# A two-layer transformer step on one core: when three side stages of a software-pipelined kernel are issued

## The chip, the cores and the metric

The kernel runs on 1 core of one Trainium2 chip. The metric is the device time of one execution in microseconds. Five engines run their own instruction streams and meet at semaphores: PE (TensorE, matmuls; PEld is its weight load), DVE (VectorE), ACT (ScalarE), POOL (GpSimd) and SP (SyncE, which only issues DMAs).

## What is computed

Sixteen sequences of 256 tokens with 128 features pass through two layers. The reference, cut to what matters:

```python
# layer 0
xn = _layernorm(x)
s = attention(xn, Wq, Wk, Wv, Wo) + bo            # 16 heads of 64, causal softmax
idx = top_k(xn @ router, 1)                        # one of 8 experts for each token
routed = (silu(g*xn @ w1[e]) * (g*xn @ w3[e])) @ w2[e]
shared = (silu(xn @ ws1) * (xn @ ws3)) @ ws2
x = x + s * silu(shared + routed)
# layer 1
xn = _layernorm(x)
s = linear_attention(xn, ...)                      # 16 heads of 8, running sums over tokens
f = xn
for l in range(2):                                 # 8 heads of 64, window 64, rotary
    f = f + local_attention(shift(f) @ wqkv[l]) @ wo[l]
    f = f + glu(layernorm(shift(f)) @ w1[l]) @ w2[l]
x = x + s * silu(f)
```

Everything is float32.

## The kernel before

The tokens form 8 blocks `b` of 512 tokens (4 tiles of 128). The work of all blocks is laid out by `Plan.lay_out` on a common list of 322 *ticks*. A tick holds at most one attention *step* (a pair of heads for one of the two sequences of a block: kind 0 is layer 0's causal attention, kind 1 the local attention of layer 1) and a list of *side stages*. Each engine's program walks the same ticks. The order inside a tick is fixed for each engine:

- PE: `produce` (queries and keys of coming pairs: L554 for kind 0, L564 transposes for kind 1), `logits` of the tick (L574 to L587), `transposes` of the probabilities of the tick before (L595), the side stages, `values` of the tick two before (L615 for kind 1, L629/L632 for kind 0), and for every second step `merge` (L639).
- ACT: evacuation of `produce` (q, k at L849), its half of the transposed probabilities (L886), the side stages, `exps` of the tick (L871, L872), evacuation of `merge` (rT at L849).
- DVE: `masked` of the tick (L1041, reads the logits from PSUM), its half of the transposed probabilities (L1052), reciprocal (L1058), `scaled` (L1063), the side stages.
- POOL: `expand` (L1341) and then the side stages; SP: side stages that are plain DMAs.

An engine issues in order, so where a side stage stands in the list decides what waits behind it. PSUM banks are handed out in rings of two (`mm`, `s`, `pt`, `o`), in the order in which the stages stand in the plan.

The side stages that the change touches:

- `("v", b, half, t)`: the value projection of layer 0 for tile `t` and one half of the heads. PE: one 128x512 matmul (L545; the profile counts two records for each). ACT: one evacuation into `v0` (L849). For each block there are 4 tiles of half 0 and 4 of half 1. They need `xnT` of the block and must be there before the first `values` of that half.
- `("r", b)`: POOL issues four indirect DMAs (L1377) that gather the routed experts' results of the block's tokens from DRAM into `r`, which is the same buffer as `xn0`. Only `down0` reads it.
- `("down0", b)`: the down projection of the shared expert. PE: 12 matmuls (L672, 24 records); DVE adds `r` and evacuates the bank (L1094).
- `("comb", b)`: ACT takes a tanh of that sum (L915, waits for L1094); DVE forms `x + s * silu(...)` in three operations one after the other (L1100, L1102, L1104), which wait for the tanh.

`f0` and `f1` are the first ticks of the block's attention for half 0 and half 1, `c` is the tick of `down0`, `late` is 4 for blocks 3 to 6 and 0 for the others, `XRING` is 3. Blocks come 36 ticks apart from block 3 on: `f0` is 81, 117, 153, 189, 225 for blocks 3 to 7, `f1` is 97, 133, 169, 205, 241, and `c` is 116, 152, 188, 224 for blocks 3 to 6. Around them stand the side stages of layer 1 of the block ahead: `lin`, `qkv` with `mix`, `rot` and `rr` (DVE: L1227, L1231, L1236, then a chain of small operations; POOL: L1395 to L1402, L1456, L1457), `kn` (L1327), `kv` (POOL L1441, L1445), `ln2`, `ln2n` (DVE, ends with L315 on `h`), `yT` (PE L540, waits for that) and `glu` (L774, L776).

## Time and profile before

| | |
|---|---|
| median of 3 runs | 2084.16 us (2081.3 to 2085.23) |
| profiled execution | 2096.84 us, span 2095.0 us |
| mean granted TensorE clock | 0.918 |
| PE busy | 1780.8 us, 85% of the span |
| DVE busy | 1283.2 us, 61% |
| ACT busy | 1186.3 us, 57% |
| POOL busy | 868.5 us, 41% |
| PE's share of the chain that ended last | 48% |
| DVE's share of it | 20% |

Busy time is summed over one profiled execution. The chain is followed back from the last instruction to whatever released each step. Positions in the trace are microseconds from the start of the span. Tick 116 is at about 810, tick 117 at 820, tick 124 at 854 and tick 134 at 914 us; the same places of the next blocks lie some 232 us further on each.

### The profile page before, as it was taken

The numbers are of one execution on the slowest core, as the hardware profiler recorded it, in microseconds if no ns is written. First come the engines' busy times: TensorE is split into PE (matmuls) and PEld (weight loads), VectorE is DVE, ScalarE is ACT, GpSimd is POOL, SyncE is SP. The second block draws the span as 40 slices with busy tenths as digits, with TensorE's granted clock in tenths as the row PEclk, the third lists the DMA queues.
The fourth block names the chain that finished last, engine by engine and source line by source line (L and its number), as shares of the span: only waits on it lengthen the run. The fifth ranks groups of instructions, "written<-read, shape, count | busy, mean of one in ns | idle before, by whom it ended". The sixth has DMA issues, their size and how long they took to land.

```text
span 2095.0 us, 38065 instructions
## 1 busy us (share of the span) xinstructions
PE 1780.8 (85%) x12532; PEld 1150.7 (55%) x12532; DVE 1283.2 (61%) x4211; ACT 1186.3 (57%) x3527; POOL 868.5 (41%) x993
## 2 busy tenths in 40 slices
PE   6679988998989888998889988988889897785876
PEld 4358754654566455664565456554556455463554
DVE  4434446556675567566756566656756656868663
ACT  2444547565756575657656675657556565553643
POOL 2633215533535334432544344533553345646410
PEclk9889999999999999999999999999999998898978
DMA  8146600000000000000000000000000000000000
GB/s 230 52 157 208 193 16 1 11 1 1 6 2 16 1 1 6 6 12 1 6 1 17 1 1 6 16 1 1 6 2 11 0 6 1 1 7 0 1 1 11
DMA packets 49725, 53.48 MB, mean 26 GB/s; under 512 B 6387, under 2 KB 42237, under 8 KB 49533
## 3 DMA queue, kind: packets, MB, share of 16 engines
q0 software_dynamic: 7808, 27.79, 4.0%
q1 hardware_dynamic: 41724, 23.26, 3.9%
q8 instruction: 104, 1.70, 0.3%
q14 instruction: 89, 0.72, 0.1%
HBM read 41.60 MB, written 9.44 MB: 24 GB/s over the span
## 4 chain that ended last, share of the span: by engine, by line
PE 48%; DVE 20%; ACT 7%; issue 6%; POOL 1%; DVEq 0%; ACTq 0%; POOLq 0%
PE ps L595 5%; PE ps L657 4%; PE ps L554 3%; PE ps L732 3%; PE ps L574 3%; DVE p L1041 3%; DVE big L1231 3%; PE ps L615 3%; PE ps L629 2%; PE ps L639 2%; DVE ss L1227 2%; PE ps L564 2%; PE ps L783 2%; PE ps L774 2%; PE ps L776 2%
## 5 line engine op out<-in xcount | busy, mean ns | idle before, releaser
L1341 POOL COPY rdx<-rden 128x256 f32<-128x256 f32 x256 | 100.8, 423 | 659.0 <-DVE rden L1058 633.9
L1041 DVE CUSTOM_DVE_ANT_0 p<-ps,mask 128x128 f32<-128x128 f32 (+1 forms) x512 | 152.2, 353 | 222.7 <-PE ps L587 216.5
L1041 DVE CUSTOM_DVE_ANT_0 p<-ps,mask,nrq 128x128 f32<-128x128 f32 x512 | 148.8, 346 | 189.1 <-PE ps L583 188.3
L595 PE MATMUL ps<-ident,p 128*128 128x128 f32 x1280 | 223.8, 300 | 27.0 <-ACT p L872 25.2
L871 ACT ACTIVATE p<-p,nmax 128x128 f32<-128x128 f32 x512 | 200.2, 391 | 52.9 <-DVE nmax L1041 52.6
L872 ACT ACTIVATE p<-p,nmax 128x128 f32<-128x128 f32 (+1 forms) x512 | 226.2, 442 | 0.0
L886 ACT ACTIVATE pt<-ps 128x384 f32<-128x384 f32 (+1 forms) x256 | 111.7, 436 | 195.8 <-PE ps L595 194.3
L732 PE MATMUL ps<-wqkv,hT 128*128 128x512 f32 x384 | 197.2, 622 | 27.5 <-ACT big L951 25.8
L595 PEld LDWEIGHTS ps<-ident,p 128*128 128x128 f32 x1280 | 146.4, 149 | 106.6 <-issue 91.0
L574 PE MATMUL ps<-k,q 64*128 64x128 f32 x1024 | 132.1, 335 | 45.1 <-DVE nmax L1041 24.2
L574 PEld LDWEIGHTS ps<-k,q 64*128 64x128 f32 x1024 | 82.0, 194 | 148.6 <-issue 85.3
L1052 DVE COPY pt<-ps 128x384 f32<-128x384 f32 (+1 forms) x256 | 124.4, 486 | 59.0 <-PE ps L595 58.9
L564 PE MATMUL ps<-ident,big 128*128 128x128 f32 x512 | 86.5, 308 | 80.2 <-DVE big L1236 37.1
L1456 POOL TENSOR_TENSOR big<-big,rots 128x512 f32<-128x512 f32 x64 | 98.1, 1533 | 124.5 <-ACT big L951 124.5
L554 PE MATMUL ps<-xnT,w 128*128 128x512 f32 x256 | 148.3, 665 | 0.9 <-ACT v L849 0.9
L615 PEld LDWEIGHTS ps<-pt,v 128*64 128x64 f32 (+1 forms) x2048 | 107.2, 138 | 71.7 <-issue 49.7
L615 PE MATMUL ps<-pt,v 64*64 64x64 f32 (+2 forms) x2048 | 143.2, 258 | 0.2 <-PE ps L615 0.2
L732 PEld LDWEIGHTS ps<-wqkv,hT 128*128 128x128 f32 x384 | 62.9, 190 | 129.3 <-ACT big L951 77.9
L657 PE MATMUL ps<-wo,attT 128*128 128x128 f32 x1024 | 125.1, 282 | 7.5 <-DVE nmax L1041 5.1
L657 PEld LDWEIGHTS ps<-wo,attT 128*128 128x128 f32 x1024 | 120.9, 197 | 12.9 <-DVE nmax L1041 9.4
L849 ACT ACTIVATE rT<-ps 128x512 f32<-128x512 f32 x128 | 74.8, 584 | 82.0 <-PE ps L639 81.4
L564 PEld LDWEIGHTS ps<-ident,big 128*128 128x128 f32 x512 | 65.2, 158 | 96.8 <-issue 68.7
(255 smaller groups left out, 4151.0 us busy)
## 6 DMA issues: line engine op xcount, KB each, us to landing
slots_in<-xn SPq DMA_DIRECT2D x1, 2560.0 KB, 14.3
v<-slots_in SPq DMA_DIRECT2D x20, 128.0 KB
slots_out<-v SPq DMA_DIRECT2D x20, 128.0 KB
big<-in_x SPq DMA_DIRECT2D x4, 512.0 KB, 6.0
x<-in_x SPq DMA_DIRECT2D x8, 256.0 KB, 3.9
out_x<-x SPq DMA_DIRECT2D x8, 256.0 KB, 2.3
wqkv<-in_wqkv SPq DMA_DIRECT2D x2, 768.0 KB
xn<-in_x SPq DMA_DIRECT2D x6, 256.0 KB, 3.1
```

The source lines that it names most:

```text
L554: MM(bank[:, :], c.wqk[which][:, a:a + P], c.xnT[:, st.b % 2, :], start=True, stop=True).then_inc(c.mm_full, 1)
L564: last = nc.tensor.transpose(bank[:, t * P:(t + 1) * P], c.qkr[:, t, a:a + P], c.ident[:, :])
L574: MM(banks[h][:, 0:P], q[f:f + HD, 0:P], k[f:f + HD, 0:P], start=True, stop=True)
L595: last = nc.tensor.transpose(bank[:, j * P:(j + 1) * P], c.p[:, u % 4, j * P:(j + 1) * P], c.ident[:, :])
L615: last = MM(bank[f:f + HD, q + at:q + end], v[keys, 2 * st.s + t, a:a + HD], pts[h][keys, at:end], **flags)
L657: last = MM(bank[:, t * P:(t + 1) * P], c.attT[kind][:, i, t * P:(t + 1) * P], w, start=i == 0, stop=i == END)
L732: MM(bank[:, :], c.hT[:, t * P:(t + 1) * P], c.wqkv[:, l, i * INNER1:(i + 1) * INNER1], start=True, stop=True).then_inc(c.mm_full, 1)
L871: A(p[:, 0:P], p[:, 0:P], ACT.Exp, bias=c.nmax[:, u % 4, 0:1], scale=-1.0, accum_out=den[:, 0:1])
L872: A(p[:, P:end], p[:, P:end], ACT.Exp, bias=c.nmax[:, u % 4, 1:2], scale=-1.0, accum_out=den[:, 1:2])\
L886: A(c.pt[:, u % 4, 0:end], c.pt_ps[pt.slot("t", st.n, 1)][:, 0:end], ACT.Copy).then_inc(c.pt_done_act, 1)
L1041: last = V.tensor_tensor_reduce(out=c.p[:, u % 4, a:b], in0=bank[:, a:b], in1=mask, scale=scale, scalar=3e38, op0=ALU.add, op1=ALU.min, ac ...
L1052: V.tensor_copy(c.pt[:, u % 4, 0:end], bank[:, 0:end]).then_inc(c.pt_done, 1)
```

## The change

Three kinds of side stage are put in other ticks. No instruction is added or removed.

```diff
             for t in range(TILES):
                 if b:
-                    self.put(f0 - (2 if b < XRING else 11 - t // 2), "v", b, 0, t)
-                self.put(f1 - 3 if b < XRING else f0 - 1 if t < 2 else f0 + 7, "v", b, 1, t)
+                    self.put(f0 - (2 if b < XRING else 11 - t // 3), "v", b, 0, t)
+                self.put(f1 - 3 if b < XRING else f0 + 6 if t < 2 else f1, "v", b, 1, t)
...
-            while any(c - 3 - late <= y and x <= c + 1 for x, y in busy) or any(c - 2 <= y and x <= c for x, y in held):
+            ahead = 6 if late else 2
+            while any(c - 3 - late <= y and x <= c + 1 for x, y in busy) or any(c - ahead <= y and x <= c for x, y in held):
...
-            held.append((c - 2, c))
-            self.put(c - 2, "r", b)
+            held.append((c - ahead, c))
+            self.put(c - ahead, "r", b)
             self.put(c, "down0", b)
-            self.put(c + (late > 0), "comb", b)
+            self.put(c, "comb", b)
```

In ticks, for the blocks that it reaches:

| stage | before | now | blocks |
|---|---|---|---|
| `v`, half 0, tile 2 | f0-10 (107, 143, ...) | f0-11 (106, 142, ...) | 3 to 7 |
| `v`, half 1, tiles 0, 1 | f0-1 (116, 152, ...) | f0+6 (123, 159, ...) | 3 to 7 |
| `v`, half 1, tiles 2, 3 | f0+7 (124, 160, ...) | f1 (133, 169, ...) | 3 to 7 |
| `r` | c-2 (114, 150, ...) | c-6 (110, 146, ...) | 3 to 6 |
| `comb` | c+1 (117, 153, ...) | c (116, 152, ...) | 3 to 6 |

The ticks of `down0` and of every attention step stay. The lines of the changed file stand one further down than those of the file before, so L672 is L673 there.

PE in ticks 116 and 117, before (the down projection of the shared expert, then two value projections):

```order
L595 MATMUL ps<-ident,p 128x128 x4
L672 MATMUL ps<-sh,ff 128x128 x12
L545 MATMUL ps<-w,xnT 128x512 x2
L615 MATMUL ps<-pt,v 64x64 x2
L615 MATMUL ps<-pt,v 64x128 x2
L615 MATMUL ps<-pt,v 64x64 x4
L639 MATMUL ps<-ident,rdx 128x128 x4
L564 MATMUL ps<-ident,big 128x128 x4
```

and in the change:

```order
L596 MATMUL ps<-ident,p 128x128 x4
L673 MATMUL ps<-sh,ff 128x128 x12
L616 MATMUL ps<-pt,v 64x64 x2
L616 MATMUL ps<-pt,v 64x128 x2
L616 MATMUL ps<-pt,v 64x64 x4
L640 MATMUL ps<-ident,rdx 128x128 x4
L565 MATMUL ps<-ident,big 128x128 x4
```

The two value projections between the down projection and `values` are gone from here.

DVE in ticks 117 and 118, before (the end of `masked` of tick 117, then `scaled` at L1063, `comb`, and `masked` of tick 118):

```order
L1041 ISA p,nmax<-ps,mask 128x256
L1041 ISA nmax 128x1
L1052 COPY pt<-ps 128x256
L1058 RECIPROCAL rden<-den 128x8
L1063 TENSOR_TENSOR attT<-ps,rT 128x512
L1100 SCALAR_TENSOR_TENSOR ff<-ff 128x512
L1102 TENSOR_TENSOR ff<-ff,s_sb 128x512
L1104 SCALAR_TENSOR_TENSOR x<-ff,x 128x512
L1041 ISA p,nmax<-ps,mask 128x128
```

and DVE in ticks 116 and 117 in the change (L1328 is `kn`, L1095 `down0`):

```order
L1328 TENSOR_TENSOR big<-big,rr 128x512 x4
L1095 TENSOR_TENSOR ff<-ps,xn 128x512
L1101 SCALAR_TENSOR_TENSOR ff<-ff 128x512
L1103 TENSOR_TENSOR ff<-ff,s_sb 128x512
L1105 SCALAR_TENSOR_TENSOR x<-ff,x 128x512
L1042 ISA p,nmax<-ps,mask 128x128
L1042 ISA nmax 128x1
L1042 ISA p,nmax<-ps,mask 128x256
```

The three operations of `comb` now stand between `down0` and `masked` of tick 117 rather than between `scaled` of tick 117 and `masked` of tick 118. On ACT the tanh stands ahead of the `exps` of tick 116 rather than ahead of those of tick 117.

PE in ticks 123 and 124, before (L595 are the transposes of ticks 122 and 123, L540 is `yT`, L740 a running sum of the linear attention):

```order
L595 MATMUL ps<-ident,p 128x128 x4
L540 MATMUL ps<-ident,h 128x128 x4
L740 MATMUL ps<-big,tri 128x288
L545 MATMUL ps<-w,xnT 128x512 x2
L615 MATMUL ps<-pt,v 64x64 x2
L615 MATMUL ps<-pt,v 64x128 x2
```

and in the change:

```order
L596 MATMUL ps<-ident,p 128x128 x4
L546 MATMUL ps<-w,xnT 128x512 x2
L616 MATMUL ps<-pt,v 64x64 x2
L616 MATMUL ps<-pt,v 64x128 x2
L616 MATMUL ps<-pt,v 64x64 x4
L575 MATMUL ps<-k,q 128x128 x2
L581 MATMUL ps<-k,q 64x64 x4
L584 MATMUL ps<-k,q 64x128 x2
L596 MATMUL ps<-ident,p 128x128 x4
L541 MATMUL ps<-ident,h 128x128 x4
L741 MATMUL ps<-big,tri 128x288
L616 MATMUL ps<-pt,v 64x64 x2
```

Two value projections (now those of tiles 0 and 1) stand ahead of `values`, `logits`, `transposes` and `yT`; none stands behind `yT` any more. Ticks 133 and 134 change in the same way, except that nothing is taken away behind their `yT`.

## Rows read from the trace of the kernel before

**Rows 1.** The page: engines' busy time, and the chain by engine.

```profile
PE 1780.8 (85%) x12532; PEld 1150.7 (55%) x12532; DVE 1283.2 (61%) x4211; ACT 1186.3 (57%) x3527; POOL 868.5 (41%) x993
...
PE 48%; DVE 20%; ACT 7%; issue 6%; POOL 1%; DVEq 0%; ACTq 0%; POOLq 0%
```

**Rows 2.** Timeline, ticks 116 to 119: start, length, engine, line, operation, [idle before, releaser].

```profile
816.37 0.69 DVE L1094 TENSOR_TENSOR ff<-ps,xn 128x512 f32<-128x512 f32 x1 [0.97 <-PE ps L672]
...
818.58 0.39 ACT L871 ACTIVATE p<-p,nmax 128x128 f32<-128x128 f32 x1
...
820.97 0.29 DVE L1041 CUSTOM_DVE_ANT_0 p<-ps,mask 128x128 f32<-128x128 f32 x1 [3.91 <-PE ps L587]
...
822.68 0.74 POOL L1341 COPY rdx<-rden 128x256 f32<-128x256 f32 x2 [16.58 <-DVE rden L1058]
...
823.09 0.88 DVE L1100 SCALAR_TENSOR_TENSOR ff<-ff 128x512 f32<-128x512 f32 x1
...
823.38 2.67 POOL L1441 TENSOR_TENSOR big<-qkb,v 128x1152 f32<-128x1152 f32 x1
...
824.00 2.60 DVE L1102 TENSOR_TENSOR ff<-ff,s_sb 128x512 f32<-128x512 f32 x1
...
826.63 0.69 DVE L1104 SCALAR_TENSOR_TENSOR x<-ff,x 128x512 f32<-128x512 f32 x1
...
827.91 0.40 ACT L871 ACTIVATE p<-p,nmax 128x128 f32<-128x128 f32 x1 [2.17 <-DVE nmax L1041]
...
830.30 0.66 PE L564 MATMUL ps<-ident,big 128*128 128x128 f32 x4 [3.06 <-ACT rT L849]
```

**Rows 3.** The chain that ended last, at 816 us: start, length, what.

```profile
816.33 1.72 PE ps L545 x4
```

**Rows 4.** One line's instructions: duration ns min/median/max, first and last start.

```profile
L1102 DVE TENSOR_TENSOR ff<-ff,s_sb x7: 691/2598/2605, 391.0 to 1721.5; 128x512 f32<-128x512 f32 x7
```

**Rows 5.** Timeline, PE in tick 83, where no `comb` stands near.

```profile
599.79 0.44 PE L564 MATMUL ps<-ident,big 128*128 128x128 f32 x2 [0.78 <-ACT rT L849]
```

**Rows 6.** Stretches: length, busy time of PE, PEld, DVE, ACT, POOL (x), granted clock.

```profile
832.00:834.00 2.00, 2.00 (x10) 1.33 (x10) 2.00 (x11) 0.76 (x3) 0.36 (x2) 0.50 0.04 8
```

**Rows 7.** Timeline, PE in tick 124.

```profile
858.35 0.63 PE L540 MATMUL ps<-ident,h 128*128 128x128 f32 x4 [2.99 <-DVE h L315]
...
859.94 3.24 PE L545 MATMUL ps<-w,xnT 128*128 128x512 f32 x4 [0.26 <-ACT xT L968]
```

**Rows 8.** Stretch in tick 124, columns as in Rows 6.

```profile
860.00:862.00 2.00, 2.00 (x3) 0.97 (x4) 0.00 (x0) 0.13 (x1) 1.66 (x3) 0.50 0.05 12
```

**Rows 9.** Timeline, PE in tick 134.

```profile
918.18 1.08 PE L540 MATMUL ps<-ident,h 128*128 128x128 f32 x4 [2.82 <-DVE h L315]
```

**Rows 10.** Stretches in tick 134 and after, columns as in Rows 6.

```profile
918.00:920.00 2.00, 1.82 (x8) 1.25 (x10) 1.97 (x12) 0.69 (x2) 0.00 (x0) 0.50 0.00 0
...
922.00:924.00 2.00, 2.00 (x6) 0.94 (x5) 0.00 (x0) 0.95 (x2) 0.00 (x0) 0.51 0.00 0
```

**Rows 11.** Timeline, PE in ticks 106 and 107.

```profile
743.93 1.09 PE L564 MATMUL ps<-ident,big 128*128 128x128 f32 x4 [3.62 <-DVE big L1236]
...
747.87 2.89 PE L545 MATMUL ps<-w,xnT 128*128 128x512 f32 x4
```

**Rows 12.** Timeline, POOL in ticks 110 to 112.

```profile
767.24 0.86 POOL L1402 TENSOR_SCALAR mn<-qkb 128x256 f32<-128x256 f32 x1
771.45 0.74 POOL L1341 COPY rdx<-rden 128x256 f32<-128x256 f32 x2 [3.35 <-DVE rden L1058]
...
779.62 0.73 POOL L1395 TENSOR_TENSOR qkb<-qkb,lb 128x256 f32<-128x256 f32 x1 [2.96 <-DVE qkb L1199]
```

**Rows 13.** Timeline, DVE in tick 112.

```profile
782.03 1.30 DVE L1236 TENSOR_TENSOR big<-big 128x1024 f32<-128x1024 f32 x1
```

**Rows 14.** Groups by line: busy us, mean ns of one, idle before.

```profile
L1236 DVE TENSOR_TENSOR big<-big 128x1024 f32<-128x1024 f32 x64 | 106.3, 1660 | 2.2
```

**Rows 15.** One line's instructions, columns as in Rows 4.

```profile
L1377 POOL DMA_INDIRECT xn<-slots_out,pos_i x32: 940/955/1891, 284.3 to 1702.4; - x32
```

More of the change, by code:

```diff
@@ L266, in lay_out @@
                 at = max(f1, self.end[(1, b - XRING, 1, PAIRS - 1)] + 12)
-                assert at <= c - 2, (b, at, c)
+                assert at <= c - ahead, (b, at, c)
                 self.put(at, "xres", b)
             shared[b] = c - 1
-            held.append((c - 2, c))
-            self.put(c - 2, "r", b)
+            held.append((c - ahead, c))
+            self.put(c - ahead, "r", b)
             self.put(c, "down0", b)
-            self.put(c + (late > 0), "comb", b)
+            self.put(c, "comb", b)
             busy.append((c - 3 - late, c + 1))
```

## The prediction

> **What bounds the kernel now.** I read the page first: PE is busy 85% of the span and carries 48% of the chain that ended last, DVE another 20% [rows 1]. So the engine that matters is mostly PE, and what can be won is its idle time, the time in which it runs at half clock, and stretches in which it does work that could lie in an idle gap. I then went through one period of 36 ticks (the block in flight is 3, then 4) in the timeline, tick by tick, and marked each wait of PE, what ended it, and the granted clock after it. The moved stages stand at four kinds of place.
>
> In tick 116, `down0` is followed by two value projections. PE works on without a pause, and they are on the chain with 1.72 us [rows 3]. DVE, done with `down0`'s eviction at 817.06 (816.37 + 0.69), waits 3.91 us for the logits of tick 117 [rows 2]. Then, when it is wanted, DVE does `comb`: 823.09 to 827.32, four microseconds of which L1102 takes 2.60 [rows 2]. Only then come the masks of tick 118; ACT has idled 2.17 us for them and starts the exponentials at 827.91, evacuates rT after them, and PE, which needs that bank, stands 3.06 us until 830.30 [rows 2]. In tick 83, the same place three ticks after the matching `kn` but without a `comb`, that wait is 0.78 us [rows 5]. After the 3.06 us the clock is granted at 0.50 for a while, which is the 1.2 GHz level [rows 6].
>
> In tick 124, PE waits 2.99 us for `h` from the layernorm chain on DVE, then does `yT`, and then two value projections that take 3.24 us, since the clock is at 0.50 there [rows 7, 8]. In tick 134 the same wait is 2.82 us, and the clock is 0.50 to 0.51 for some six microseconds after it [rows 9, 10]. In tick 106, two projections precede a wait of 3.62 us for DVE, and the other two follow in tick 107, in 2.89 us at the low clock [rows 11].
>
> **The change, part by part.** A projection costs PE 0.86 us at full clock (1.72 for two [rows 3]). The count of projections stays, so each term is: what leaves the chain where it stood, less what it adds where it goes.
>
> *Tile 2 of half 0, tick 107 to 106 (5 blocks).* It joins the two that stand before a wait of 3.62 us [rows 11], which ends by DVE alone; the gap becomes 2.76 us. Added: nothing. Removed behind it: 0.86 us, and not half of 2.89, since I take the low clock to last as long as before, with other work in it. 5 x 0.86 = 4.3 us.
>
> *Tick 116 to 119 (4 blocks).* Two steps at once. Without the projections PE has the logits of tick 117 out 1.72 us earlier, at some 819.3. `comb` on ACT: the tanh may start at 817.1, when L1094 is through, and takes 0.6; the exponentials of tick 116, behind it on ACT, start at 817.7 and not at 818.58 [rows 2], where they waited for the evacuation of the projections. `comb` on DVE: L1100 from 817.8, 0.87; L1102; L1104, 0.69. For L1102 the trace has 0.691 and 2.60 [rows 4]. The slow one lies beside POOL's L1441, from 823.38 to 826.05, and ends half a microsecond after it [rows 2]. At 818 POOL is idle (it waits 16.58 us, until 822.68 [rows 2]), so I take 0.69. DVE is then free at 820.1, still before the 820.97 at which it starts masks now. The masks of tick 118 follow PE's logits, 1.5 to 1.7 us earlier than now, at about 822.8 instead of behind `comb` (827.3). ACT is free for their exponentials when it has done those of tick 117 and copied the transposes, at 824.1 by my count, against 827.91. From there to the bank that PE waits for nothing changes, so PE goes on at 826.5 instead of 830.30: 3.8 us, in which the 1.72 us are contained. 4 x 3.8 = 15.2 us. PE's wait shrinks to some 0.7 us, like rows 5, and I take it that the clock stays up then: the low stretch of 3.4 us is filled with PE's work, which at full clock takes half, 1.6 to 1.7 us. 4 x 1.6 = 6.4 us. Bounds: without the clock 15.2; if another wait replaces DVE's, only the projections' 4 x 1.72 = 6.9.
>
> The Trainium skill (SBUF — State Buffer, § SBUF: two separate sides) says that a DVE operation with two SBUF inputs and a GpSimd operation that reads SBUF exclude each other for whole instructions, whichever starts first. By that rule L1102 would cost 2.60 in tick 116 too if POOL ran L1441 there; the term would be 1.9 us less for each block, 7.6 in all. POOL's wait in rows 2 speaks against it.
>
> *Tiles 0 and 1 of half 1, into tick 123, and tiles 2 and 3 out of tick 124 (5 blocks).* In tick 123 the pair goes ahead of `logits` and `transposes` of tick 124 and of `yT`. `yT` waits for DVE until 858.35, of which 2.99 us are idle [rows 7], and nothing of DVE's layernorm chain waits for the pair. ACT evacuates two more tiles before the exponentials of tick 123, which start about 1.4 us later, and the transposes behind them end near 856.4, still 1.9 us before `yT`. So the 1.72 us cost nothing here. If that cover were gone they would cost 1.72 for each block, 8.6 in all. In tick 124 the pair is gone: 3.24 us of the chain [rows 7], of which 1.72 is its own work at full clock and the rest the low clock. If the clock falls as before, other work runs through the low stretch instead and 1.72 is won; if the shorter gap (some 1.9 us in place of 2.99 and a small one before) keeps it up, about 1.6 more. No row that I use shows a gap between 0.78 and 2.82 us and what the clock did after it, so I count half. 5 x 1.72 = 8.6, and 5 x 1.6 / 2 = 4.0 us.
>
> *Tiles 2 and 3 into tick 133 (5 blocks).* The same cover: a wait of 2.82 us for the same chain of DVE [rows 9] against 1.72 us. Cost 0. If the clock stays up after the shorter gap, the 6 us at 0.50 [rows 10] shrink to some 3.3 (ACT's exponentials take part of the room), 2.7 us. Half again: 5 x 2.7 / 2 = 6.7 us.
>
> *Tiles 0 and 1 out of tick 80 (block 3).* No `comb` stands there and DVE sets what follows. 0.
>
> *`r` four ticks up (4 blocks).* POOL issues four gathers of 0.94 to 1.9 us each (median 0.955 [rows 15]), with gaps 5 to 6.5 us in all. In tick 110 they come behind L1402, done at 768.1. Behind them on POOL: `expand`, `lin` and `qkv` of the next ticks; for these DVE waits last at 782.03 [rows 13]. POOL has idle 3.35 + 2.96 = 6.3 us in ticks 111 and 112 [rows 12], so it has caught up at 779.6, or 0.2 us later. Where `r` leaves (tick 114), nobody waits for POOL. Cost 0 to 0.4 us a block; I take 0. SP's queue is untouched.
>
> Sum: 4.3 + 15.2 + 6.4 + 8.6 + 4.0 + 0 + 6.7 = 45.2 us. The profiled execution takes 2096.84 us and would come to 2051.6. The median of the runs shown is 12.7 us lower; I carry the same 45 us over: 2084.16 - 45 = 2039 us.
>
> **The rivals.**
>
> *The clock comes back nowhere.* Shorter gaps still end in the low level. Then 4.3 + 15.2 + 8.6 = 28 us: 2056. For it: every wait of PE of 2.8 us or more in my rows is followed by it; the new gaps of 1.9 us are in between.
>
> *The clock stays up everywhere,* in ticks 134 and 124 too: 45.2 + 4.0 + 6.7 = 56 us: 2028; with tick 107 as well, 5 x 1.6 more: 2020.
>
> *Another wait replaces DVE's in tick 118.* ACT's queue (tanh before the exponentials) or a bank is late next; the term is 6.9 instead of 21.6, and with little clock back it comes to about 20 us: 2064. Against it: ACT's 2.17 us of idle and the 0.78 us of rows 5.
>
> *The projections are not hidden.* If the pairs in ticks 123 and 133 lengthen the ticks through ACT (two evacuations ahead of the exponentials, then transposes ahead of `yT`), 5 x 2 x 1.72 = 17 us come back. On top of a replaced wait and an unchanged clock (20 us won) 3 us are left: 2081.
>
> *Slower: `r` makes POOL late.* If the gathers take more than the 6.3 us that POOL has, L1456 and L1457 meet DVE's L1231 and L1236 in all four tiles of `qkv`. L1236 takes 1.30 us when it meets little [rows 13] and 1.66 in the mean [rows 14], so the met ones cost about 1 us more; 4 tiles x 2 operations x 1 us = 8 us, in a stretch in which DVE sets the end. That is 4 x 8 = 32 us against the 28 us without clock (PE would wait longer, so none comes back): 2084 + 4 = 2089. It decides from 7 us a block. The skill's rule above is the same lock. Against it: POOL's idle time covers the median gather.
>
> **How the numbers follow.** Forecast 0.42; clock nowhere 0.22; clock everywhere 0.16; wait replaced 0.10; not hidden 0.06; slower 0.04. The likeliest is 2039. The range takes in the first four: 2021 to 2066. About 0.2%, 4 us, is what a measurement of this kernel can tell from no change. Faster by more: 0.90; within: 0.06; slower by more: 0.04.
>
> **What would show it.** In the profile of the changed kernel: L1103 (L1102 in the file before) near 0.69 us for blocks 3 to 6 and before the masks of tick 117; PE's wait for rT in tick 119 below 1 us; some 10 us less from one `down0` to the next than before; the waits for `h` near 1.9 us; and the granted clock after these. Wrong would be: L1103 at 2.6, the waits for `h` gone or `yT` later than its DVE chain, the four gathers longer than 6.5 us, or waits of DVE on POOL in ticks 112 to 116.

## The result, and the profile after

The changed kernel takes 2065.58 us (median of 4 runs, 2061.76 to 2066.93) beside 2084.65 us for the kernel before (4 runs, 2081.3 to 2085.23): ratio 0.9906, 95% interval 0.9893 to 0.9919. It is 19 us faster. The forecast was 45 us faster, 2039, with a range that ended at 2066. Less than half of the gain came.

The profiled execution of the changed kernel takes 2066.93 us, 29.9 us less than that of the kernel before (2096.84). So 11 of the missing 26 us come from the base and not from a term of the sum: the profiled execution of the kernel before, from which the terms were read, was 12 us slower than its own median, and that of the change is about 1 us slower than its. The page of the changed kernel, the same rows as in [rows 1]:

```profile
PE 1775.8 (86%) x12532; PEld 1147.0 (56%) x12532; DVE 1275.1 (62%) x4211; ACT 1185.6 (57%) x3527; POOL 858.2 (42%) x993
...
PE 47%; DVE 20%; ACT 7%; issue 6%; POOL 1%; DVEq 0%; ACTq 0%; POOLq 0%
```

PE does the same instructions and is busy 5 us less; a second profile of the kernel before (same_again, below) has 1766.8 us, so this difference says little. DVE is busy 8.1 us less, 7.6 of it in L1102. POOL is busy 10.3 us less: 1.8 in the four L1441 that had met L1102, and 6.9 in the gathers:

```profile
L1378 POOL DMA_INDIRECT xn<-slots_out,pos_i x32: 940/947/1050, 286.0 to 1673.5; - x32
```

In tick 114 the first and the fourth gather of a block had taken 1.85 and 1.89 us; in tick 110 none takes more than 1.05, and the four of block 3 are through in 4.8 us. (Lines of the changed file stand one further down.)

**Ticks 116 to 119.** One line's instructions (duration ns min/median/max, first and last start), and then the timeline of ticks 116 to 119 in the changed kernel (start, length, engine, line, operation, idle before and its releaser):

```profile
L1103 DVE TENSOR_TENSOR ff<-ff,s_sb x7: 691/692/693, 389.7 to 1692.0; 128x512 f32<-128x512 f32 x7
```

```profile
818.29 0.69 DVE L1095 TENSOR_TENSOR ff<-ps,xn 128x512 f32<-128x512 f32 x1 [1.29 <-PE ps L673]
...
820.40 0.69 DVE L1103 TENSOR_TENSOR ff<-ff,s_sb 128x512 f32<-128x512 f32 x1
...
824.65 0.29 DVE L1042 CUSTOM_DVE_ANT_0 p<-ps,mask 128x128 f32<-128x128 f32 x1 [0.72 <-PE ps L588]
...
828.24 0.66 PE L565 MATMUL ps<-ident,big 128*128 128x128 f32 x4 [0.78 <-ACT rT L850]
```

The last of the three operations of `comb` ends at 821.8, 0.7 us after PE's logits of tick 117, so the masks of tick 117 start a little later for it. It does not reach PE: ACT works on without a pause there, and DVE then waits 0.72 us for the logits of tick 118. In blocks 3 to 6 L1103 takes 0.69 us where [rows 4] had 2.60. PE's wait for rT is 0.78 us in place of 3.06 [rows 2]. This is the row that the prediction asked for, to the hundredth of [rows 5]; it is the same in blocks 3 to 6, and no low stretch follows it in any of them. From one `down0` to the next the profile shows 6.9 us less than that of before, where the prediction had some 10. The granted clock behind the wait is 1.00, where [rows 6] had 0.50 (stretch, length, busy time of PE, PEld, DVE, ACT, POOL with counts, granted clock, DMA):

```profile
830.00:832.00 2.00, 2.00 (x20) 1.52 (x19) 2.00 (x11) 1.45 (x6) 0.42 (x2) 1.00 0.04 8
```

From here on the clock "falls behind a wait" when a stretch at 0.50 begins within the wait or at most 1.8 us after its end.

**Ticks 106 to 109.** Timeline of PE in the changed kernel:

```profile
744.07 0.63 PE L565 MATMUL ps<-ident,big 128*128 128x128 f32 x4 [2.60 <-DVE big L1237]
...
746.90 1.92 PE L546 MATMUL ps<-w,xnT 128*128 128x512 f32 x2
...
751.66 1.47 PE L565 MATMUL ps<-ident,big 128*128 128x128 f32 x8 [2.05 <-DVE big L1328]
```

The wait of [rows 11] shrank from 3.62 to 2.60 us, and behind it a second wait of 2.05 us stands that the prediction did not have: PE now has only one projection in tick 107 and is early for `kn` (L1328), which DVE finishes when it did. Both waits end by DVE, and the distance from the first to the second is 7.59 us. Behind the second wait the clock falls once more:

```profile
752.00:754.00 2.00, 2.00 (x13) 1.67 (x13) 0.00 (x0) 1.19 (x2) 0.00 (x0) 0.54 0.00 0
```

**Ticks 124 and 134.** Timeline of PE and the granted clock behind each, in the changed kernel:

```profile
854.73 1.08 PE L541 MATMUL ps<-ident,h 128*128 128x128 f32 x4 [1.73 <-DVE h L316]
...
912.26 0.78 PE L541 MATMUL ps<-ident,h 128*128 128x128 f32 x4 [1.55 <-DVE h L316]
```

```profile
856.00:858.00 2.00, 2.00 (x16) 1.07 (x14) 0.00 (x0) 1.82 (x7) 0.65 (x1) 0.50 0.01 4
914.00:916.00 2.00, 2.00 (x11) 1.36 (x8) 1.30 (x5) 1.94 (x9) 0.00 (x0) 0.50 0.00 0
916.00:918.00 2.00, 2.00 (x10) 1.15 (x9) 0.93 (x3) 1.34 (x3) 0.20 (x1) 1.00 0.00 0
```

The waits are 1.73 and 1.55 us in place of 2.99 [rows 7] and 2.82 [rows 9]. The clock still falls to 0.50 behind both in this block; over the five blocks it falls five times in tick 124 and three times in tick 134. `yT` itself keeps its place: in all 17 profiled executions of the table below it starts 5.90 to 5.94 us after the masks of tick 123 and 6.06 to 6.09 us after those of tick 133, in all five blocks.

**Time by place.** I took the start of DVE's masks (L1041, L1042 in the changed file) in every tick as the clock of the program, and measured four segments: ticks 106 to 110, 116 to 121, 124 to 126 and 134 to 137, and the same of the later blocks. The table gives the mean of blocks 4 to 7 in us, one profiled execution for each kernel; the period is a quarter of the time from tick 101 to tick 245. The runs of the next section are in it. The ratio is the recorded one, against runs of the kernel before from the same session; it can differ from the quotient of the two medians by up to 0.0018, or nearly 4 us. The sessions ran on different chips, so kernels of different sessions are compared by their ratios.

| kernel | 106-110 | 116-121 | 124-126 | 134-137 | period | ratio to before (95%) |
|---|---|---|---|---|---|---|
| before | 25.8 | 33.1 | 17.6 | 22.4 | 232.1 | |
| same_again | 25.8 | 33.1 | 17.4 | 20.3 | 229.6 | 0.9998 (0.9976-1.002) |
| the change | 27.3 | 28.1 | 16.0 | 20.8 | 225.2 | 0.9906 (0.9893-0.9919) |
| change_again | 27.3 | 27.8 | 15.2 | 21.3 | 225.3 | 0.9908 (0.9876-0.9941) |
| tile2_back | 25.8 | 27.6 | 16.0 | 20.5 | 222.8 | 0.9813 (0.9782-0.9845) |
| tile2_back_2 | 25.8 | 27.5 | 15.3 | 20.8 | 223.3 | 0.9832 (0.9814-0.985) |
| tile2_only | 27.5 | 33.8 | 17.6 | 21.3 | 233.4 | 1.0059 (1.0038-1.008) |
| comb_only | 25.8 | 29.1 | 17.8 | 22.5 | 228.3 | 0.9932 (0.991-0.9954) |
| proj_only | 25.8 | 32.3 | 16.8 | 21.0 | 228.8 | 0.994 (0.9919-0.9961) |
| r_back | 27.3 | 27.9 | 16.0 | 20.8 | 225.2 | 0.9879 (0.9844-0.9914) |
| tile2_r_back | 26.1 | 27.8 | 16.0 | 20.5 | 223.4 | 0.9834 (0.9809-0.9858) |
| one_three | 26.2 | 28.2 | 16.8 | 20.3 | 225.3 | 0.9882 (0.9848-0.9916) |
| half1_115_123 | 25.8 | 26.9 | 15.2 | 20.8 | 222.0 | 0.9867 (0.9847-0.9888) |
| half1_115_133 | 25.8 | 27.2 | 16.5 | 20.3 | 223.7 | 0.9858 (0.9839-0.9878) |
| fill_107 | 26.5 | 27.8 | 14.9 | 21.3 | 224.1 | 0.9842 (0.9818-0.9866) |
| fill_124_134 | 25.8 | 27.9 | 13.8 | 20.3 | 221.4 | 0.9778 (0.9756-0.9801) |
| fill_all | 25.8 | 28.2 | 13.8 | 20.3 | 221.8 | 0.98 (0.9771-0.9828) |

Against the profiled execution of before, a period is 6.9 us shorter, four of them 28. Against same_again, which is the same kernel in another execution, it is 4.4 us shorter, four of them 17 to 18. The first is near what the two profiles differ by (30), the second near what the medians differ by (19). Up to tick 65, where none of these kernels differs from another, the profiled executions took 475 to 482 us: whole spans of single profiles say little, and the segments are what can be compared.

### The profile page after: what moved, and what is told of

Its sections match the earlier page's. It is cut to its first block, busy times and chain, and to the rows that moved or that the text cites. A ratio compares the mean times of both kernels' runs of the same rounds, so it can differ in the third digit from the quotient of the medians.

```text
span 2065.1 us, 38065 instructions
## 1 busy us (share of the span) xinstructions
PE 1775.8 (86%) x12532; PEld 1147.0 (56%) x12532; DVE 1275.1 (62%) x4211; ACT 1185.6 (57%) x3527; POOL 858.2 (42%) x993
## 4 chain that ended last, share of the span: by engine, by line
PE 47%; DVE 20%; ACT 7%; issue 6%; POOL 1%; DVEq 0%; ACTq 0%; POOLq 0%
PE ps L596 5%; PE ps L658 5%; PE ps L616 3%; PE ps L733 3%; PE ps L555 3%; PE ps L575 3%; DVE p L1042 3%; DVE big L1232 3%; PE ps L640 2%; PE ps L630 2%; PE ps L775 2%; PE ps L784 2%; DVE ss L1228 2%; PE ps L565 2%; PE ps L777 2%
## 5 line engine op out<-in xcount | busy, mean ns | idle before, releaser
L1042 DVE CUSTOM_DVE_ANT_0 p<-ps,mask 128x128 f32<-128x128 f32 (+1 forms) x512 | 152.2, 353 | 215.0 <-PE ps L588 208.8
L1042 DVE CUSTOM_DVE_ANT_0 p<-ps,mask,nrq 128x128 f32<-128x128 f32 x512 | 148.9, 347 | 176.8 <-PE ps L584 176.0
L733 PE MATMUL ps<-wqkv,hT 128*128 128x512 f32 x384 | 196.8, 622 | 26.5 <-ACT big L952 26.5
L565 PE MATMUL ps<-ident,big 128*128 128x128 f32 x512 | 82.2, 297 | 76.5 <-DVE big L1237 34.2
L850 ACT ACTIVATE k<-ps 128x512 f32<-128x512 f32 x128 | 74.8, 585 | 76.8 <-PE ps L555 41.5
```

Source lines behind the costliest of these rows:

```text
L565: last = nc.tensor.transpose(bank[:, t * P:(t + 1) * P], c.qkr[:, t, a:a + P], c.ident[:, :])
L733: MM(bank[:, :], c.hT[:, t * P:(t + 1) * P], c.wqkv[:, l, i * INNER1:(i + 1) * INNER1], start=True, stop=True).then_inc(c.mm_full, 1)
L850: A(dst, mm_bank(*name)[:, :], ACT.Copy).then_inc(c.mm_done, 1)
L1042: last = V.tensor_tensor_reduce(out=c.p[:, u % 4, a:b], in0=bank[:, a:b], in1=mask, scale=scale, scalar=3e38, op0=ALU.add, op1=ALU.min, ac ...
```

## The experiments

The theory on which the runs were planned: in ticks 106 to 109 the change took away what covered PE's wait for `kn`; in ticks 124 and 134 the clock's part of the gain was counted too high; `comb` worked as forecast. The rival: all of the missing gain is the difference between one execution and the next.

**The kernel before again** (no edit).

> The kernel before, unchanged, timed and profiled once more. It is for the base: its profiled execution took 2096.84 us where the runs had a median of 2084.65, while the changed kernel's profiled execution (2066.93) lies among its runs. If that profile was merely long, this one comes to about 2084 to 2086, with the same waits of PE and fewer or shorter stretches at half clock. If a profile of this kernel is always 12 us longer, it comes to about 2097 again.

Measured: 2092.36 us against 2093.0 in the same session. The profiled execution has a span of 2084.3 us, against 2095.0 for that of before, so the profile of before was merely a long one (that of same_again, 2086.12 us, is one of the short ones of its session). The difference stands in tick 134. Timeline of PE and the granted clock behind it, in same_again:

```profile
918.23 0.63 PE L540 MATMUL ps<-ident,h 128*128 128x128 f32 x4 [2.82 <-DVE h L315]
```

```profile
918.00:920.00 2.00, 1.77 (x16) 1.31 (x17) 1.97 (x12) 1.10 (x4) 0.00 (x0) 1.00 0.00 0
920.00:922.00 2.00, 1.87 (x11) 0.97 (x9) 1.80 (x7) 2.00 (x9) 0.00 (x0) 1.00 0.00 0
```

The same wait of 2.82 us as in [rows 9], and the clock stays at 1.00, where [rows 10] had 0.50, in all five blocks. The segment takes 20.25 us with the clock up and 22.4 with the fall. So the prediction's 6.7 us for tick 134 rested on falls that belong to the execution and not to the kernel.

**Tile 2 of half 0, back in the change, and alone in the kernel before.**

```diff
  # tile2_back: the change with
-                    self.put(f0 - (2 if b < XRING else 11 - t // 3), "v", b, 0, t)
+                    self.put(f0 - (2 if b < XRING else 11 - t // 2), "v", b, 0, t)
  # tile2_only: the kernel before with
-                    self.put(f0 - (2 if b < XRING else 11 - t // 2), "v", b, 0, t)
+                    self.put(f0 - (2 if b < XRING else 11 - t // 3), "v", b, 0, t)
```

> The changed kernel, but tile 2 of half 0 back in tick 107 (two and two, as before). Theory (lost cover): in tick 108 PE needs the last operation of kn on DVE (L1328), which ends at the same time in both kernels; the projections of tick 107 lay over that wait. With one of them gone PE waits 2.05 us and the clock falls a second time. Putting it back removes wait and fall in four blocks, 4 x 1.57 = 6.3 us: about 2059. Rival (the move is worth its 0.86 us and the loss in the step times has another cause, such as the shifted banks): 5 x 0.86 longer, 2070.

> The kernel before with only tile 2 of half 0 moved from tick 107 to 106. Lost cover: slower by 4 x 1.57 less about 0.8 in block 3, some 5 us: 2090, with waits of about 2 us in tick 108 of blocks 4 to 7. By the prediction's term: 4.3 us faster, 2080.

Measured: tile2_back 2054.14 us, tile2_only 2103.42, before 2093.0. Both effects are larger than expected. Beside 2093.0 the change would be at some 2073 us (0.9906 of it); the theory took 6.3 us off that, and 19 came off. tile2_only was to lose 5 us and lost 10 in the medians, 12 by the ratio. Undoing this one line makes the change 16 to 20 us faster (0.9813 and, in a later session, 0.9832, against 0.9906 and 0.9908), and doing it alone makes the kernel before 10 to 12 us slower. PE in ticks 107 and 108 of tile2_back, and the clock behind:

```profile
743.59 0.63 PE L565 MATMUL ps<-ident,big 128*128 128x128 f32 x4 [3.62 <-DVE big L1237]
...
746.44 2.78 PE L546 MATMUL ps<-w,xnT 128*128 128x512 f32 x4
...
751.18 1.06 PE L565 MATMUL ps<-ident,big 128*128 128x128 f32 x8 [1.15 <-DVE big L1328]
```

```profile
752.00:754.00 2.00, 2.00 (x19) 1.34 (x19) 0.87 (x7) 0.99 (x3) 0.00 (x0) 1.00 0.02 4
```

From 743.59 to 751.18 is 7.59 us again. In the kernel before, where PE started at 743.93 [rows 11], the same operation follows 7.59 us behind as well, and with no wait, since two projections at the low clock had filled the time:

```profile
751.52 1.06 PE L564 MATMUL ps<-ident,big 128*128 128x128 f32 x8
```

So the wait itself costs nothing: PE resumes at the same point, since DVE sets it. What differs is what follows, 1.06 us at full clock here, 1.47 in the change, and 27.3 instead of 25.8 us to the masks of tick 110. "Lost cover" told only half of it; the experiment after next tells the rest.

**Split turned round**: one projection in tick 106, three in tick 107.

```diff
-                    self.put(f0 - (2 if b < XRING else 11 - t // 3), "v", b, 0, t)
+                    self.put(f0 - (2 if b < XRING else 10 + (t == 0)), "v", b, 0, t)
```

> The change with the split of half 0 turned round: one projection in tick 106, three in tick 107. Theory (what stands in tick 107 covers the time until kn is done, two projections are just enough, and the wait of tick 106 is free for any number): the third projection in tick 107 has no wait left to lie in and costs 0.86 us for each of 5 blocks, while the 1.57 us and the second fall of the clock of the change are gone. So tile2_back plus 4 us: 0.983 of before. Rival (the change's loss has to do with tick 106, where three evacuations stand ahead of other work of ACT, and not with the cover): one in tick 106 is then better still than two, 0.980 or less. No wait of PE for kn in tick 108 by the first.

Measured: 0.9882. Ticks 106 to 110 take 26.2 us, half a us more than with two and two (PE now comes 0.6 us too late: 744.22 to 752.40 is 8.18 us), and there is no second fall of the clock in any block. That speaks for tick 107 and against ACT's queue in tick 106, but the whole kernel lost more against tile2_back (10 to 14 us) than these 0.5 x 5 us; in its profile tick 124 to 126 sits at 16.8 us and ticks 110 to 112 are 0.7 us longer. The expected 0.983 was missed, as was the rival's 0.980 or less; where the rest went is open.

**The same work in the wait, by PE alone.** The change with one matmul done twice into its bank; nothing else moves, and the result is the same.

```diff
         bank = mm_bank("v", b, half, t, 0)
+        if b >= XRING and (half, t) == (0, 3):
+            MM(bank[:, :], c.xnT[:, b % 2, t * P:(t + 1) * P], c.wv[:, half * 512:(half + 1) * 512],
+               start=True, stop=True)
         MM(bank[:, :], c.xnT[:, b % 2, t * P:(t + 1) * P], c.wv[:, half * 512:(half + 1) * 512],
```

> The change, with the matmul of half 0's tile 3 in tick 107 done twice into its bank (PE only, 0.86 us more work for each of blocks 3 to 7, same result). PE then has as much work in tick 107 as in the kernel before, while nothing but that is changed. Theory (the wait for kn ends by DVE at the same place in every kernel, 7.59 us behind the wait of tick 107; what the change lost there is the second fall of the clock behind the longer wait): the wait is 1.15 us, there is no second fall, ticks 106 to 110 take 25.7 instead of 27.2 us, and the kernel with more work is faster than the change: 0.984 to 0.987 of before. Rival (it is the work itself or its place in ACT's and DVE's queues): the added 4.3 us cost nothing or all of it, 0.991 to 0.993.

Measured: 2056.9 us, 0.9842 (0.9818 to 0.9866), against 0.9906 and 0.9908 without the added work. By the ratios a kernel that does more is 13 us faster. Its profile shows 0.8 us less a block in this segment and 1.1 in the period, so most of the 13 us are not located. PE in ticks 107 and 108 of fill_107, and the clock behind:

```profile
736.60 0.63 PE L568 MATMUL ps<-ident,big 128*128 128x128 f32 x4 [2.60 <-DVE big L1240]
...
740.06 1.31 PE L547 MATMUL ps<-w,xnT 128*128 128x512 f32 x2
741.21 1.02 PE L549 MATMUL ps<-w,xnT 128*128 128x512 f32 x2
...
744.19 1.06 PE L568 MATMUL ps<-ident,big 128*128 128x128 f32 x8 [1.16 <-DVE big L1331]
```

```profile
744.00:746.00 2.00, 1.81 (x16) 1.38 (x16) 0.05 (x1) 1.70 (x6) 0.00 (x0) 1.00 0.00 0
746.00:748.00 2.00, 2.00 (x19) 1.47 (x18) 1.67 (x9) 1.05 (x4) 0.00 (x0) 1.00 0.01 4
```

(The file's lines stand up to three further down.) From 736.60 to 744.19 is 7.59 us for the fourth time. The wait for `kn` is 1.16 instead of 2.05 us here and 1.10 to 1.16 in blocks 3 to 5, and the clock stays up behind it. In blocks 6 and 7 it falls, but there the wait is not 1.16 us long:

```profile
1190.10 1.06 PE L568 MATMUL ps<-ident,big 128*128 128x128 f32 x8 [3.13 <-DVE big L1331]
```

It is 3.13 us in block 6 and 2.79 in block 7. In these two blocks the clock had not fallen behind the first wait, so PE did tick 107 at full clock, was early for `kn`, and the clock fell behind the second wait instead. Over the 17 profiled executions (85 blocks) the second wait was 1.51 us or less in 63 blocks, with no fall behind it in any, and 2.00 us or more in 22, with a fall in all. Those 22 are 19 of the 20 blocks of the four kernels with three projections in tick 106 and one in 107 (the change, change_again, r_back, tile2_only), two of fill_107, and one of the 50 with two and two (block 7 of tile2_r_back, 2.78 us, again after full clock in tick 107). With two projections' work in tick 107 and no second fall, ticks 106 to 110 take 25.7 to 25.8 us (26.05 in block 6), whether the low stretch behind the first wait lasts 3.4 or 6.8 us; with the second fall they take 27.0 to 27.6 in blocks 4 to 7 (27.95 once), also where the clock had not fallen behind the first. So there a fall behind the first wait costs nothing, since DVE sets when tick 108 starts, and a fall behind the second costs some 1.5 us.

**The waits for `h` filled in the same way.** tile2_back, with tiles 1 and 3 of half 1 done twice (ticks 123 and 133); fill_all adds tile 3 of half 0. (The first line stands in fill_124_134, the second in fill_all.)

```diff
+        if b >= XRING and half and t % 2:                        # fill_124_134
+        if b >= XRING and t % 2 and (half, t) != (0, 1):         # fill_all
```

> tile2_back, with the matmuls of half 1's tiles 1 and 3 done twice (ticks 123 and 133, 0.86 us more each ahead of yT, whose end by DVE isn't touched). The waits for h shrink from 1.73 and 1.57 to 0.87 and 0.7 us. Theory (length of PE's wait decides whether the clock falls): no fall behind either, tick 124 to 126 take 13.8 us in all blocks (16.0 in the mean now) and 134 to 137 take 20.25 (20.5 to 20.8 now): 4 x 2.4 = 10 us less than tile2_back, 0.977 to 0.979. Rival (the clock falls there by something else, as it fell and did not fall behind the same waits): no less, 0.982 to 0.984.

> tile2_back, with tile 3 of half 0 (tick 107) and tiles 1 and 3 of half 1 done twice. In tick 107 the wait for kn goes from 1.15 to 0.3 us. There was no second fall in 10 of 10 blocks of tile2_back, so both theories expect nothing more there: the time of fill_124_134 within 2 us. If it is slower by 4 us, a filling of that wait costs its own time.

Measured: fill_124_134 2046.85 us, 0.9778, as its theory had it; fill_all 2049.47, 0.98 (the two intervals overlap). tile2_back, without the repeats, has 0.9813 and 0.9832 from two other sessions; the interval of the first overlaps too, that of the second does not. PE in ticks 124 and 134 of fill_124_134, and the clock behind each:

```profile
847.10 0.63 PE L541 MATMUL ps<-ident,h 128*128 128x128 f32 x4 [0.86 <-DVE h L316]
...
903.19 0.63 PE L541 MATMUL ps<-ident,h 128*128 128x128 f32 x4 [0.69 <-DVE h L316]
```

```profile
848.00:850.00 2.00, 2.00 (x22) 1.50 (x22) 0.37 (x3) 2.00 (x9) 1.02 (x2) 1.00 0.05 12
850.00:852.00 2.00, 2.00 (x23) 1.20 (x22) 0.47 (x3) 1.34 (x4) 1.92 (x4) 1.00 0.00 0
904.00:906.00 2.00, 2.00 (x15) 1.21 (x12) 1.93 (x9) 2.00 (x8) 0.00 (x0) 1.00 0.00 0
```

In the two kernels the clock falls in none of ten blocks in either place, and the segments stand at 13.76 and 20.25 us in every block. With waits of 1.7 and 1.55 us (nine profiled kernels with the projections as in the change, 45 blocks) it fell 40 times in tick 124 and 22 times in tick 134. Fill_124_134 has the lowest median of all kernels here, with 20 more matmul records than the change. A repeat is free only while a wait is left for it: in block 3 of fill_all the projections of tick 107 ran at the low clock, no wait was left, and the transposes of tick 108 came 8.45 us after those of tick 107 instead of 7.59.

**`comb` alone, and the projections of half 1 alone**, in the kernel before.

```diff
  # comb_only
-            self.put(c + (late > 0), "comb", b)
+            self.put(c, "comb", b)
  # proj_only
-                self.put(f1 - 3 if b < XRING else f0 - 1 if t < 2 else f0 + 7, "v", b, 1, t)
+                self.put(f1 - 3 if b < XRING else f0 + 6 if t < 2 else f1, "v", b, 1, t)
```

> The kernel before with only comb moved, from the tick after down0 into its own. Theory: this alone takes DVE's three operations out of the way of the masks of tick 118. PE's wait for rT in tick 119 falls from 3.06 us to below 1, L1102 takes 0.69 us, and the clock does not fall there: 4 x (3 + 1.6) = 18 us, 2066. Rival (comb has to wait behind the two projections' evacuations on ACT and blocks the masks of tick 117 instead): at most 4 x 1 us, 2081.

> Of the change only the projections of half 1 are moved (ticks 116 to 123 and 124 to 133); comb, r and tile 2 of half 0 stay. Theory (each pair that leaves a busy place and goes into a wait of PE is worth its own 1.72 us, and the clock sometimes): 4 x 1.7 in tick 116, 7 in tick 124, 8 in tick 134, together 22 us less than before, 0.9895. Rival (the 39 us of tile2_back are mostly from comb, and the projections only work together with it): 8 to 12 us less, 0.995. In its profile the wait of PE for rT in tick 119 should still be some 3 us.

Measured: comb_only 14 us less than before (0.9932; the theory's figure was 0.991, the rival's 0.998), proj_only 14.5 us less in the medians (0.994, near the rival's 0.995 and not the theory's 0.9895). One line and PE's wait in tick 119, first of comb_only and then of proj_only:

```profile
L1102 DVE TENSOR_TENSOR ff<-ff,s_sb x7: 691/692/693, 391.9 to 1703.5; 128x512 f32<-128x512 f32 x7
825.21 0.66 PE L564 MATMUL ps<-ident,big 128*128 128x128 f32 x4 [0.77 <-ACT rT L849]
```

```profile
816.16 2.60 DVE L1102 TENSOR_TENSOR ff<-ff,s_sb 128x512 f32<-128x512 f32 x1
822.47 1.11 PE L564 MATMUL ps<-ident,big 128*128 128x128 f32 x4 [3.06 <-ACT rT L849]
```

`comb` alone takes the wait away and brings 4.0 us of the segment 116 to 121; the projections alone leave it at 3.06 us and bring 0.8 there, less than their own 1.72, since `comb` sets what follows, and in tick 124 also less (0.6 to 0.9 us in place of some 1.6, with a long low stretch in each block). Both together bring 5.4 to 5.6 (tile2_back, tile2_back_2). By the ratios the two bring 14 and 12.6 us alone and 35 together (tile2_r_back, 0.9834, which has just these two), so some 8 us come only with both. L1102 takes 0.69 us in every block once `comb` stands in tick 116, where POOL is idle, and 2.60 in blocks 3 to 6 where it stays in tick 117 beside POOL's L1441. The Trainium skill (SBUF — State Buffer, § SBUF: two separate sides) says that a DVE operation with two SBUF inputs and a GpSimd operation that reads SBUF exclude each other for a whole instruction, and that the one that starts first goes through. The traces agree.

**`r` back at c-2**, in the change and in tile2_back.

```diff
-            self.put(c - ahead, "r", b)
+            self.put(c - 2, "r", b)
```

> The change with r at c-2 as before. Theory (the gathers cost nothing in either place, POOL has idle time around both): the time of change_again within 2 us, ratio 0.9906 give or take 0.001. Rival (the four gathers in tick 110 delay qkv's operations of POOL and so DVE in ticks 111 to 114): 4 to 8 us less than change_again, 0.987 to 0.989. Or the other sign: r in tick 114 meets down0 and comb, up to 4 us more.

> Half 1 and comb as in the change, tile 2 of half 0 and r as before. Theory (the four gathers in tick 110 delay DVE's masks and ACT's copy of the next tick by some 0.6 us in a block where they do): 0 to 3 us less than tile2_back_2, ticks 110 and 111 at 5.60 and 8.00 us in all four blocks. Rival (the 6.6 us between r_back and change_again are r's): 6 us less.

Measured: r_back 2063.72 against 2070.28 for change_again in the same session, with intervals that overlap (0.9844 to 0.9914, 0.9876 to 0.9941); tile2_r_back 2058.44 against 2055.93 for tile2_back_2, the other sign. So no effect on the time is shown. There is one in the profiles, though: ticks 110 and 111 took 13.6 us together in all blocks of the change and of tile2_back, with the gathers in tick 110, but 14.2 to 14.7 in blocks 4 to 7 of all eight kernels of the later sessions that have the gathers there (change_again, one_three, tile2_back_2, the two of half 1, the three with repeats). In the same sessions it is 13.6 with `r` in tick 114 (proj_only, r_back, tile2_r_back). Tick 74, where `r` of block 2 stands in every kernel, agrees: 6.2 us in these sessions and in the profile of before, 5.6 in that of the change and in the session of tile2_back. ACT's copy of the transposes in tick 111, in change_again and in tile2_back:

```profile
767.91 0.38 ACT L887 ACTIVATE pt<-ps 128x256 f32<-128x256 f32 x1 [2.09 <-PE ps L596]
```

```profile
770.00 0.38 ACT L887 ACTIVATE pt<-ps 128x256 f32<-128x256 f32 x1 [0.69 <-PE ps L596]
```

PE's work that is named as the releaser ended 1.4 us before ACT went on in change_again. What held it is not in the trace; with `r` in tick 114 the 0.69 stands in r_back too. So in some sessions the move of `r` costs 0.6 us or more a block, some 3 us in all; what makes it so is open.

**The change again.**

> The change itself, once more, on the chip of the three runs that follow. Both theories: 0.9906 of the kernel before, the interval within 0.989 to 0.993. It serves as the base of the other three. In its profile the wait of PE for kn in tick 108 (2.05 us) must stand again, since it follows from the order; where the clock falls in ticks 124 and 134 need not be the same as in the first profile.

Measured: 0.9908. The second fall in tick 108 stands in all five blocks.

**tile2_back again, and half 1 in other waits.** Tiles 0 and 1 in tick 115, where PE stood 3.96 us for the logits of tick 116.

```diff
-                self.put(f1 - 3 if b < XRING else f0 + 6 if t < 2 else f1, "v", b, 1, t)
+                self.put(f1 - 3 if b < XRING else f0 - 2 if t < 2 else f0 + 6, "v", b, 1, t)   # half1_115_123
+                self.put(f1 - 3 if b < XRING else f0 - 2 if t < 2 else f1, "v", b, 1, t)       # half1_115_133
```

> The change with tile 2 of half 0 back in tick 107, once more, on the chip of the three runs that follow, since one_three and r_back were compared with it across two chips. Theory (the cover in tick 107 is worth 9 us of profile in each comparison, the rest of the 15 us seen the first time was the two chips' difference): 0.984 to 0.987 of before. Rival (all 20 us seen the first time are the effect): 0.981. Whether ticks 110 and 111 take 5.60 and 8.00 us, as in the first profiles of this placement of r, or 6.1 and 8.1, as in change_again and one_three, is open.

> As tile2_back, but tiles 0 and 1 of half 1 in tick 115, where PE stands 3.96 us before the logits of tick 116, and tiles 2 and 3 in tick 123; none in tick 133. The pair changes one wait of PE for another. Theory (a pair is worth its 1.72 us in any wait of PE that is longer than itself): tick 134 has its 2.82 us again and loses 1.1 to 2.2 us a block, ticks 115 and 116 take no longer: net 0 to 5 us either way of tile2_back_2, apart from the clock. Rival (behind the attention's output projection in tick 115 a pair delays DVE's masks of tick 116, so that it isn't hidden): 4 x 1.7 = 7 us more, with the 5 x 1.2 of tick 134, 13 us more.

> As half1_115_123, but tiles 2 and 3 in tick 133; none in tick 123, so that the wait for h in tick 124 is 2.99 us again. Theory: the same as half1_115_123 within 3 us, with tick 134 shorter by 1.1 and tick 124 longer by 1 to 2.5 us. If the clock falls in tick 124 after 2.99 us and doesn't after 1.73 us, half1_115_123 is ahead; by the runs so far it falls after both at most times. Rival (the wait's length decides the clock): 8 us apart.

Measured: 2055.93, 2064.74 and 2060.6 us. tile2_back_2, at 0.9832, lies between what its theory (0.984 to 0.987) and its rival (0.981) had. The pair hides in tick 115 (ticks 116 to 121 come to 26.9 and 27.2 us), but neither kernel beats tile2_back: 0.9867 and 0.9858 against 0.9832. The profile of half1_115_123 is of its fastest run (2050.1 us), so it can't show where its median of 2064.74 is lost. Neither the theory (within 5 us of tile2_back_2) nor the rival (13 us more) is borne out by its 9 us.

## Why the prediction was right and wrong

**`comb` and the projections out of tick 116: right.** Forecast 5.4 us a block, 15.2 + 6.4 in all; measured 5.0 (33.1 to 28.1). L1103 at 0.69, the wait at 0.78 and the clock at 1.00 came as written. comb_only shows that most of it is `comb`, and that the two parts help each other. The rival of another wait in DVE's place is out by the 0.78 us, that of a late POOL by the gathers of 4.8 us and the unchanged ticks 110 and 111 (its own sum has a slip: 2084 + 4 is 2088).

**Tile 2 of half 0: wrong in sign, and the largest miss.** The failed step is "Removed behind it: 0.86 us". It took the two projections of tick 107 to be on the path, because they follow a wait and run at the low clock. But PE waits for DVE again in tick 108, or, in the profile of before, arrives just in time: the transposes of tick 108 start 7.59 us after those of tick 107 (7.94 in block 6) with one projection between, with two, and with one that is done twice. DVE was the bound through the whole stretch, from L1236 to `kn`, so no work of PE could be won there, and the work that was moved out was what kept PE's second wait short. Instead of 4.3 us less it cost some 1.5 us in each of four blocks, 6 us in the profile, by the second fall of the clock. In the run times the line is worth 10 to 12 us alone and 16 to 20 in the change; the profiles of tile2_back account for 8 to 10 of these, and the rest is not located.

**Ticks 124 and 134: the right mechanism, the terms too large.** The cover held: the waits shrank and `yT` came no later, which also answers the rival of projections that are not hidden. Tick 124 gave 1.4 to 1.6 us a block instead of 2.5. The failed step is "count half" for the clock: behind a wait of 1.73 us it fell in 40 of 45 blocks. With one low stretch the segment takes 15.2 us, with a longer one 16.8, without 13.76; the kernels with the old order always had 17.3 to 18.0. In tick 134 the term was for the clock alone (6.7 us), and half the base was missing: of 20 blocks with the old 2.82 us, the clock fell in 11 and the segment took 22.4 to 22.5 us, and it took 20.25 in the 9 others; with 1.55 us it took 21.2 to 21.4 or 20.25. What differs is the low stretch: with 22.4 it began some 1.1 us before the end of the wait and lasted 6.8 us, with 21.3 it began later and lasted 3.4. half1_115_123 has the wait of 2.82 us and the shorter stretch, and 21.36 us, in two of its blocks. So the shorter wait is worth at most 1.1 us where the clock falls and nothing where it doesn't, and the fall is about as frequent. Behind [rows 9] stood no work of PE that could be saved, since DVE sets `yT`.

**The base.** "I carry the same 45 us over" failed by 11 us. Gains from the clock were priced on an execution with 343.7 us of low clock (sum of the low stretches); same_again had 282.2, and the change 294.4 in the one profile and 277.4 in the other. Read from the profile of same_again, with its period of 229.6 us, the term of tick 134 would have been near zero.

**`r`, tick 80:** nothing, as forecast, in the profile of the change; in later sessions `r` in tick 110 cost 0.6 us or more a block, a little above the 0 to 0.4 that the prediction allowed.

In sums for a period of four blocks: forecast 0.9 + 5.4 + 2.5 + 1.3 = 10.1 us; measured against same_again -1.5 + 5.0 + 1.4 - 0.5 = 4.4. The likeliest rival, "the clock comes back nowhere" (2056), was nearer, and still too low for the 1.5 us that it counted as 0.9 won. The rival nearest in number is 2064, with another wait in DVE's place, and its mechanism did not occur. That the result lies just inside the range (2021 to 2066) is therefore luck: the range reached so far for that rival.

The clock fell behind single waits of 1.55 us (22 of 45 blocks), 1.73 us (40 of 45) and 2.00 us and more in front of tick 108 (22 of 22), and not behind 1.51 us or less there or 0.87 us or less in ticks 124 and 134. The Trainium skill (TensorE: Matmul & The Clock Gate, § A second HAM failure mode: psum-queue depth-cycling) tells of another kernel in which frequent short idles of PE between groups of matmuls made the clock swing between its two levels. The traces agree in kind, with the counts above. Why the fall comes in one block and not in the next behind the same wait is not shown.

## What to carry to other kernels

Before an operation is taken out of a stretch for its length, follow the engine to its next wait: if the same other engine ends both waits, everything between them is free, a low clock included, and it may be what holds the matmul clock up behind the second. Where PE waits for another engine anyway, a repeated matmul that still fits into the wait costs nothing and can keep the clock up: two repeats a block took the ratio from 0.981 to 0.983 down to 0.978 here. And gains that hang on the clock need at least two profiled executions of the base, since the same kernel differs by some 60 us of low clock between two of them.

## What was not expected of the hardware

- The length of low clock belongs to the execution as much as to the kernel: 343.7 and 282.2 us in two profiles of the kernel before, all five blocks of each alike behind the wait of 2.82 us (a fall in five of five in one, in none of five in the other).
- More work can be less time: five matmuls of some 0.9 us each, added in a wait, made the kernel 13 us faster by the ratios (0.9907 to 0.9842).
- The length of a wait goes with the fall in one place and not in another: in front of tick 108 the clock fell in none of 63 blocks with at most 1.51 us of waiting and in all 22 with 2.00 us or more; in tick 134 it fell behind 22 of 45 waits of 1.55 us and stayed up behind 9 of 20 of 2.82 us. Below 0.9 us in ticks 124 and 134 it fell in none of twenty places.
- A stretch at the low clock can cost nothing. Behind the first wait of ticks 106 to 109 it lasted 3.4 or 6.8 us, or was not there at all, and with at most two projections in tick 107 the transposes of tick 108 started 7.59 us after those of tick 107 in each case (7.94 in block 6).
- With four gathers of POOL in tick 110, ACT and DVE started an operation of the next tick 0.5 to 1.4 us later than the work they are shown to wait for, in some sessions and not in others. The cause is open.
